# A ring of four for the key scales and of eight for the keys, and exponentials nearer to their use, in the second cross attention

## The reference, cut to what matters

```python
q = rmsnorm((layernorm(x) @ Wq).reshape(B, 32, 16, 128), gq)
k = rmsnorm((ctx @ Wk).reshape(B, 257, 16, 128), gk)
v = (ctx @ Wv).reshape(B, 257, 16, 128)
attn = softmax(einsum("bqhd,bkhd->bhqk", q, k) / sqrt(128))
x = x + einsum("bhqk,bkhd->bqhd", attn, v).reshape(B, 32, 2048) @ Wo
```

## Time and profile before

| | us |
|---|---|
| median of 3 runs | 3049.93 (3046.38 to 3054.54) |
| the profiled execution, its own time | 3047.74 |
| its span in the profile | 3045.9 |
| of it up to the second cross attention | 1340 |
| second cross attention, to the next block's first load | 822 |
| what follows | 884 |

### The profile page before, as it was taken

The page is one execution under the profiler, slowest core; times in us unless marked ns, Lnnn a source line. Parts: engine busy times, 40 slices in busy tenths (PEclk is TensorE's granted clock), DMA queues, the critical chain, the costliest instruction groups (busy, mean ns, idle before and its releaser), DMA issues. The chain is left out here.

```text
span 3045.9 us, 49566 instructions
## 1 busy us (share of the span) xinstructions
PE 2772.8 (91%) x13964; PEld 2090.3 (69%) x13964; DVE 1419.1 (47%) x4720; ACT 1342.5 (44%) x4875; POOL 681.2 (22%) x867
## 2 busy tenths in 40 slices
PE   6999999798999999887887788788799999997999
PEld 5888888686444444455665566556588888886887
DVE  3665455575777444444444444443133333332433
ACT  2555445465666666535334433444222222221333
POOL 1333222264455200142223222301500000000000
PEclk8999999899999999999999999999899999998999
DMA  5222111201400243134234422313600000000000
GB/s 166 61 61 66 48 48 47 102 0 37 148 5 1 75 119 112 43 95 130 79 80 106 119 63 70 93 59 109 128 15 0 0 0 0 0 0 28 11 7 10
DMA packets 158157, 178.12 MB, mean 58 GB/s; under 512 B 31884, under 2 KB 125513, under 8 KB 157411
## 3 DMA queue, kind: packets, MB, share of 16 engines
q1 hardware_dynamic: 131730, 148.13, 16.6%
q0 software_dynamic: 13824, 25.23, 3.9%
q10 hardware_dynamic: 12496, 3.57, 0.8%
HBM read 141.12 MB, written 48.28 MB: 62 GB/s over the span
## 5 line engine op out<-in xcount | busy, mean ns | idle before, releaser
L544 PE MATMUL xa_probsT_ps<-all_ident,xa_probs 128*128 128x128 f32 x1024 | 203.6, 281 | 82.8 <-ACT xa_probsT L677 77.8
L669 ACT ACTIVATE xa_probs<-xa_probs,xa_shift,xa_row_scale 128x257 f32<-128x257 f32 x256 | 152.6, 596 | 280.3 <-DVE xa_shift L794 278.6
L221 PE MATMUL rt_kn_key_ps<-moe_w_wk,all_big 128*128 128x512 f32 x560 | 248.6, 597 | 0.8 <-DVE moe_kn_stats L270 0.4
L544 PEld LDWEIGHTS xa_probsT_ps<-all_ident,xa_probs 128*128 128x128 f32 x1024 | 135.5, 144 | 162.3 <-DVE xa_probs L810 99.0
L2126 PE MATMUL sa_work_ps<-sa_xnT,all_big 128*128 128x128 f32 x2048 | 235.8, 278 | 10.3 <-ACT sa_xnT L2196 5.8
L2126 PEld LDWEIGHTS sa_work_ps<-sa_xnT,all_big 128*128 128x128 f32 x2048 | 234.1, 195 | 11.1 <-ACT sa_xnT L2196 6.1
L524 PE MATMUL xa_misc_ps<-xa_xnT,cross_folded 128*128 128x256 f32 x1024 | 232.9, 382 | 6.2 <-ACT xa_squares L653 5.6
L567 PE MATMUL xa_misc_ps<-cross_folded,xa_mixT 128*128 128x256 f32 x1024 | 229.3, 379 | 0.0
L524 PEld LDWEIGHTS xa_misc_ps<-xa_xnT,cross_folded 128*128 128x128 f32 x1024 | 194.9, 191 | 39.6 <-ACT xa_squares L653 12.2
L786 DVE CUSTOM_DVE_ANT_0 xa_probs<-xa_score_ps,xa_key_scale 128x257 f32<-128x257 f32 x256 | 105.5, 424 | 249.6 <-DMA xa_key_scale<-rk 103.1
L537 PE MATMUL xa_score_ps<-xa_pair,xa_qT 128*128 128x257 f32 x512 | 165.9, 416 | 57.0 <-DVE xa_top L786 55.2
(11 more groups left out here) (310 smaller groups left out, 5325.0 us busy)
## 6 DMA issues: line engine op xcount, KB each, us to landing
xa_key_scale<-rk SPq DMA_DIRECT2D x256, 128.5 KB
xa_pair<-pairs SPq DMA_DIRECT2D x64, 256.5 KB
pairs<-all_big SPq DMA_DIRECT2D x64, 128.5 KB, 2.9
xa_rows<-in_ctx_dram SPq DMA_DIRECT2D x64, 128.0 KB, 2.5
pairs<-xa_keys SPq DMA_DIRECT2D x64, 128.0 KB, 2.0
cross_folded<-in_L_ffn_w_gate_dram SPq DMA_DIRECT2D x32, 192.0 KB, 2.5
cross_folded<-in_L_ffn_w_up_dram SPq DMA_DIRECT2D x32, 192.0 KB, 2.7
xa_last_key<-in_ctx_dram SPq DMA_DIRECT2D x64, 64.0 KB, 3.3
```

The costliest lines, as they stand in the source:

```text
L221: pe.matmul(self.key_ps[m % self.banks][0:n, :], self.ctxT[:, c * P:c * P + n], self.wk[:, q * 512:(q + 1) * 512], start=True, stop=True). ...
L544: ins = pe.transpose(probsT_ps[s % 2][:, k * P:(k + 1) * P], probs[:, s % SR, k * P:(k + 1) * P], ident[:, :])
L669: act.activation(probs[:, s % SR, :], probs[:, s % SR, :], ACT.Exp, bias=least, scale=scale, accum_out=total[:, col]).then_inc(exped, 1)
```

## The change

In the second cross attention only (`layer` is 1): pairs have eight places (`RING` 8), key scales four (`SCALES` 4). The count of `weighed` is raised by three items' rows at the start instead of one (`PRE`), so key scales wait until the item four before is weighed. The key scales now lie in the fourth quarter of `big`, the gathered rows in the third, where wo comes later, and wv in the fourth. So the codes of wv can't be loaded during the iterations any more: SP loads them after the last row is weighed, 2 MB in four transfers. And `exp` and its `share_out` are at most four rows ahead of `turn` (`EXP_AHEAD`), while scores, weighing and shifts are still six ahead. The first cross attention keeps its numbers.

```diff
-        RING = 4
-        ROWS = 2 * RING
-        CTX_AHEAD = RING
-        EARLY = 2
+        RING, SCALES = (8, 4) if layer else (4, 2)
+        ROWS = 8
+        CTX_AHEAD = 4
+        EARLY, EXP_AHEAD = 2, 4
...
+        PRE = (SCALES - 1) * R
...
-            key_scale = sc.sb("key_scale", [P, 2, R, S2])
+            key_scale = key_scales(ctxT)
...
-                        sp.dma_start(key_scale[j * T:(j + 1) * T, b % 2, :, :].rearrange("p r s -> p (r s)"),
+                        sp.dma_start(key_scale[j * T:(j + 1) * T, b % SCALES, :, :].rearrange("p r s -> p (r s)"),
...
-                    if codes and b % 2 and b < NB - 1:
-                        after.load_codes(sp, ("wq", "wk", "wv")[b // 2], i, codes_ahead)
+                    if codes and b in (1, 3):
+                        after.load_codes(sp, ("wq", "wk")[b // 2], i, codes_ahead)
...
             items(ITERS - 1)
+            sp.wait_ge(weighed, ITERS * ST + PRE)
+            for g in range(SA_GROUPS):
+                after.load_codes(sp, "wv", g, codes_ahead)
...
-                pe.wait_ge(weighed, i * ST + (s - 1 + R))
+                pe.wait_ge(weighed, i * ST + (s - 1 + PRE))
...
-                    if s + AHEAD < ST:
-                        exp(i, s + AHEAD)
+                    if s + EXP_AHEAD < ST:
+                        exp(i, s + EXP_AHEAD)
...
-                for s in range(AHEAD):
+                for s in range(EXP_AHEAD):
                     exp(i + 1, s)
...
-                        if AHEAD <= s + EARLY < ST:
+                        if EXP_AHEAD <= s + EARLY < ST:
                             share_out(i, s + EARLY, link)
...
-                    for s in range(0, AHEAD, ROWS_AT_ONCE):
+                    for s in range(0, EXP_AHEAD, ROWS_AT_ONCE):
                         share_out(i + 1, s, link)
...
-    return ctxT[:, 3 * SA_WEIGHT:3 * SA_WEIGHT + 2 * K0 * D].rearrange("p (g k d) -> p g k d", g=2, k=K0)
+    return ctxT[:, 2 * SA_WEIGHT:2 * SA_WEIGHT + 2 * K0 * D].rearrange("p (g k d) -> p g k d", g=2, k=K0)
+
+
+def key_scales(ctxT):
+
+    R = H * T // P
+    return ctxT[:, 3 * SA_WEIGHT:3 * SA_WEIGHT + 4 * R * S2].rearrange("p (n r s) -> p n r s", n=4, r=R)
```

More of the change, by code:

```diff
@@ L405, in cross_attention @@
         ctx_turned, ctx_kept = sc.sem("ctx_turned"), sc.sem("ctx_kept")
-        kscale_loaded = [sc.sem(f"kscale_loaded{n}") for n in range(2)]
+        kscale_loaded = [sc.sem(f"kscale_loaded{n}") for n in range(SCALES)]
         keys_ready, columns_stored, keys_stored = sc.sem("keys_ready"), sc.sem("columns_stored"), [
@@ L663, in exp @@
                 if layer == 0:
-                    act.wait_ge(weighed, i * ST + s + 1 + R)
+                    act.wait_ge(weighed, i * ST + s + 1 + PRE)
                     scale, least = -1.0, top[:, col]
@@ L732, in _ @@
         def _(dve):
-            FIRST = 1 + AHEAD // ROWS_AT_ONCE
+            FIRST = 1 + EXP_AHEAD // ROWS_AT_ONCE
             LINKS = 1 + ST // ROWS_AT_ONCE
@@ L780, in weigh @@
                     if r == 0:
-                        dve.wait_ge(kscale_loaded[b % 2], i * (16 * HR * NB // 2) + 16 * HR * (b // 2 + 1))
-                    other, op, pick, start = key_scale[:, b % 2, r, :], ALU.mult, ALU.max, -3.4e38
+                        dve.wait_ge(kscale_loaded[b % SCALES], i * (16 * HR * NB // SCALES) + 16 * HR * (b // SCALES + 1))
+                    other, op, pick, start = key_scale[:, b % SCALES, r, :], ALU.mult, ALU.max, -3.4e38
                 dve.wait_ge(turned, i * ST + max(s - SR + 1, 0))
@@ L791, in shift_rows @@
                 b, r, cols = first // R, first % R, slice(first % SR, first % SR + ROWS_AT_ONCE)
-                dve.wait_ge(weighed, i * ST + (first + ROWS_AT_ONCE + R))
+                dve.wait_ge(weighed, i * ST + (first + ROWS_AT_ONCE + PRE))
                 apart(dve, passed)
@@ L867, in iteration @@
                     add(i, t)
-            dve.sem_inc(weighed, R)
+            dve.sem_inc(weighed, PRE)
             every_last = ctxT[:, S2 - 1:KEYS:S2] if layer == 0 else None
@@ L2015, in __init__ @@
         self.I = I
-        self.wq, self.wk, self.wv, self.wo = (big[:, n * SA_WEIGHT:(n + 1) * SA_WEIGHT] for n in range(4))
+        self.wq, self.wk, self.wo, self.wv = (big[:, n * SA_WEIGHT:(n + 1) * SA_WEIGHT] for n in range(4))
         self.scales = spare[:, :].rearrange("p (m c n) -> p m c n", m=SCALE_SLOTS, c=NC)
```

2 lines of the change are left out of this document (1 added, 1 removed).

## The result

The changed kernel takes 2888.8 us (median of 4 runs, 2886.39 to 2890.09), the kernel before beside it 3052.23 (4 runs, 3046.38 to 3054.63): a ratio of 0.9466, 95% interval 0.9450 to 0.9483. 2893 was predicted, in a range of 2865 to 2945. The profiled execution took 2886.39 us for a span of 2884.6, 161.3 less than the one of before; the granted TensorE clock is 0.978 of full speed over the span.

What follows compares the result with a forecast made beforehand. Waits for key scales in two places, with a PE-DVE-ACT loop beneath, bound the attention stretches. Stretches of 6 x 35.5 + 33 + 38 = 284 us for 439.1, 155 less, gave 2893 us, range 2865 to 2945.

Steps and rivals of the forecast that it cites:

- The loop of two rows in 2.90 us: Attention stretches: PE, DVE and ACT wait in a circle, 6.4 us an item with `keep_mix`; later exponentials cut it.
- PE's step of 1.10: Attention stretches after the change: turn, score and mix take PE 1.10 us a step, 33 us a stretch.
- The clock that was to be 1.00: Sign of being right: all attention stretches run at a granted TensorE clock of 1.00.
- rival 2: Attention stretches: the loop is replaced, not cut; an item stays at 6.4 us, 63 us less, 2985; chance 0.07.
- The queue passes an item in 5.9 us, and 7.5 among gathers: Key-scale and pair loads: at this pace only a stretch's eighth item is late, by 1.3 us.
- queueing against gathers: Iterations 0 to 5: the eighth item's lateness taken as 2.5 us, not 1.3, giving 35.5 us a stretch.
- The seventh stretch 33, the last 38: Iteration 6 has no gathers, 33 us; the last iteration's items follow 2 MB of scales, late by 5, 38 us.
- Codes of wv cost nothing: End of the block: 2 MB loaded after the last row is weighed, under 20 us of cover, cost 0.
- Key scales on four engines: Key-scale transfers: a slowest dimension of 4 keeps them on four engines; passing side by side would give 2873.
- the loop and the ring: Attention stretches before: loop 6.4 us an item, hidden under the key scales' two places, about 8.5 us an item.

Runs made afterwards that it cites:

- The rings alone: Changed kernel with exponentials and share_out six rows ahead as before, leaving only eight pair and four key-scale places: 3016.16 us, ratio 0.9764 to the kernel before.
- the spread: Changed kernel with the key scales' source rearranged to a slowest dimension of 16, not 4, reading two copies: 2918.53 us, ratio 0.9447 to the kernel before.
- the lag without rings: Changed kernel with four pair and two key-scale places as before, leaving only the later exponentials: 3096.82 us, ratio 1.0016 to the kernel before.
- The filler: Changed kernel with four pair and two key-scale places, plus twelve unused matmuls at three rows of each stretch: 3070.95 us, ratio 0.9933 to the kernel before.

## Why the prediction was right

*The loop of two rows in 2.90 us goes, PE's step of 1.10 is next.* Right: 1.09 between turns, 32.5 us of busy PE in a stretch and 32.7 to 34.1 us of length from the second stretch to the seventh. The rings alone show the loop by itself; I had it at 6.4 us an item, and unhindered it takes 5.7. The clock that was to be 1.00 was so in seven of the eight stretches, and 0.95 in the first. The loop through `exp(s+3)` and `share_out(s+2)` (rival 2) costs nothing that shows.

*The queue passes an item in 5.9 us, and 7.5 among gathers.* Right for the last stretch, 5.7 to 6.1 apart. With 7.5 I had the eighth item's key scales land at 27 and be wanted at 25.7; in the second, third, fourth and sixth stretch it was weighed at 27.1, 26.9, 27.0 and 26.3 after the first turn. So the position was right, and nearly the 1.3 us of lateness that it gives. The one term that was mis-sized is what I put on top, 2.5 in place of 1.3 for queueing against gathers, for which I had no row. The item was late by 0 to 1.75, 0.9 on average. (What I called the third item in the earlier trace rows is the fourth, row 12; the sum does not use its number.) Those six stretches took 36.06 + 34.06 + 33.92 + 33.95 + 32.88 + 33.35 = 204.2 us, where I had 213. This is 8.8 of the 9.1 us by which my sum of 284 missed 274.9; with 1.3 I would have had 205.8 for the six. The total came nearer, 4.2 us off, and that is luck, by what has nothing to do with the change: 2.7 us more ahead of the stage, and a median 2.4 above the profiled execution.

*The seventh stretch 33, the last 38 because its items queue behind 2 MB of scales.* Right to the number: 32.67 and 38.00. Of the reason, the spread shows that it is the rate of the queue (38.00 to 33.02 with the scales still ahead). That the scales' place ahead is the trouble was my reading, and it is half of it: with them behind, the seventh item waited 0.57 us and no longer 2.60, and the eighth lost more than that.

*Codes of wv cost nothing.* Right: 21.40 against 21.39 us.

*Key scales on four engines.* The Trainium skill, "DMA: Bandwidth & Descriptors", in the section on why a DMA increments its semaphore by 16, ties the number of engines to the slowest dimension. The runs agree: a slowest dimension of 16 in place of 4 took the share from 0.26 to 0.80. I had put the worth of this at 20 us (2893 to 2873); it measured 10.3, since the eighth items were less late than I thought and the sixth stretch lost 2.9 us of its own. That it would be worth 72.5 us in the kernel before I did not see; there it touched the binding cycle of two items.

*What I did not foresee* is that the parts don't add. I priced the loop and the ring by two bounds, of which the larger holds, and that gives no hint that one part alone gives nothing. With the lag in place, by pairs and key scales (ratios; the one with eight pairs and two key scales is from the third chip):

| | two key scales | four key scales |
|---|---|---|
| four pairs | 1.0016 | 0.9848 |
| eight pairs | 0.9854 | 0.9478 |

One ring at a time brings 1.6 to 1.7%, both 5.4%. Without the lag both bring 2.4%. For the lag without rings the rows show a reason: 10.85 us from issue to use and a hold in SP's order that the lag does not touch, and PE at half its clock after the waits shown. The filler shows the clock's part to be 26 us at least; that the hold and the landing are the rest is argued from one cycle. How the 4.8 us a stretch that stay between the filler's 52.8 and the 48 expected divide between the filler's own cost and the hold stays open.

## What to carry to other kernels

Before deepening a ring, look at the transfer: a share near 0.25 while it passes alone went here with four of sixteen engines, and another order of the source's dimensions gave what two rings gave. Transfers with different waits on one queue hold each other up: here either ring alone brought 1.6 to 1.7%, and both 5.4%. Their order decides which one waits for the other; swapping it gained with four and four places and lost with four and two, so try it on the places that you have. Where the bound is a wait, a faster loop can lengthen the wait instead of the pace, and if TensorE is what waits, its clock may take the rest, as with the lag alone.

## What the runs showed of the hardware

- After TensorE stood for 5.3 us, its next instructions ran at half speed (a score of two matmuls starting 1.01 us ahead of the mix, not 0.44, at a granted clock of 0.50), for about two steps; the granted clock of the stretches with such waits was 0.81 to 0.88. Filler matmuls in these waits brought it to 0.94 to 1.00. In the kernel before it followed a stand of 2.5 us too (the score at 1704.33, with a clock of 0.57 from 1704 to 1708).
- Issuing the four transfers of key scales takes SP 2.73 us at its quickest in the changed kernel, and 6.02 in the row shown, where four items' loads had gone out in the 17 us before. That the queue was full is my reading.
- With 2 MB issued right behind them, the last item's key scales were used 8.5 us after those of the item before; in the changed kernel on the same chip, with nothing behind them, 5.9.
- Key scales on all engines moved at 197 to 204 GB/s, on four at 104.
- Two chips differ by 1.3 to 1.4% in the whole kernel, before and after alike, and in the changed kernel by under 1 us in seven of the eight attention stretches.
